# Turning the normalised tiles of a transformer layer's fused pass by DMA instead of TensorE

## The reference

```python
h  = layernorm(x)                       # source norm
Q, K = elu(h@Wq + bq) + 1, elu(h@Wk + bk) + 1;  v = h@Wv + bv
KV = sum_s K[s] v[s]^T  per head (16 heads of 64)
Z  = 1 / (Q . sum_s K[s] + 1e-6)
t  = h + (Q KV Z)@Wo + bo
x1 = layernorm(t)*g1 + be1              # first norm
u  = x1 + gelu(x1@W1 + b1)@W2 + b2      # hidden size 4096
xa = x + layernorm(u)*g2 + be2          # second norm
n  = layernorm(xa)                      # third norm
out = xa + n@weight.T + pooled(n)@disha # folded into n@Wf
```

## Time and profile before

| | us |
|---|---|
| Median of 3 runs | 1622.37 (1622.12 to 1623.51) |
| The profiled execution's own time | 1624.31 |
| Its span, core 5, the slowest | 1622.8 (other cores from 1617.1) |
| TensorE busy | 1539.5 (95%) |
| VectorE busy | 928.4 (57%) |
| ScalarE busy | 598.4 (37%) |
| GpSimd busy | 502.7 (31%) |
| Granted TensorE clock, mean | 0.982 |

### The profile page before, as it was taken

How to read it: one execution, slowest core, us unless ns; L and a number is a source line. 1 busy time by engine, 2 the same in 40 slices (tenths; PEclk the granted TensorE clock), 3 DMA queues, 4 the chain that set the end, 5 groups by cost and what they waited for, 6 DMA issues and landing times.

```text
span 1622.8 us, 28100 instructions; the slowest of 8 cores (1617.1 to 1622.8 us)
## 1 busy us (share of the span) xinstructions
PE 1539.5 (95%) x9892; PEld 928.7 (57%) x9892; DVE 928.4 (57%) x1042; ACT 598.4 (37%) x1010; POOL 502.7 (31%) x438
## 2 busy tenths in 40 slices
PE   2699999999789999999999999999999999999995
PEld 1254544554356666666666666666666666666662
DVE  1466665665626574756657474755657475665314
ACT  1244555544533233333323333342323333332321
POOL 3464544545344222222222222222122222222101
PEclk9799999999899999999999999999999999999998
DMA  9776655457772201111110201111120111111011
GB/s 174 180 169 181 158 161 142 131 138 160 146 148 93 74 32 66 39 54 53 53 66 27 79 27 66 45 48 53 53 78 27 66 40 53 53 53 54 26 40 39
DMA packets 52183, 135.60 MB, mean 84 GB/s; under 512 B 5968, under 2 KB 14160, under 8 KB 52048
## 3 DMA queue, kind: packets, MB, share of 16 engines
q1 hardware_dynamic: 31408, 101.82, 18.7%
q0 software_dynamic: 14112, 25.70, 10.5%
q10 hardware_dynamic: 6528, 6.29, 1.3%
HBM read 117.53 MB, written 41.94 MB: 98 GB/s over the span
## 4 chain that ended last, share of the span: by engine, by line
PE 92%; issue 2%; DVE 2%; DMA 2%; POOL 1%; ACT 1%; SPq 0%; DVEq 0%; ACTq 0%; POOLq 0%
PE psH L1100 27%; PE psY L1081 27%; PE psY L444 13%; PE psS L673 7%; PE psS L493 6%; PE psS L415 6%; PE psS L659 1%; PE psS L547 1%; PE psH L423 1%; DMA qt_s<-arena 1%; PE psS L436 1%; PE psS L568 1%; DMA arena<-x 1%; PE psY L415 1%; PE psY L493 0%
## 5 line engine op out<-in xcount | busy, mean ns | idle before, releaser
L1100 PE MATMUL psH<-arena 128*128 128x256 bf16 x4096 | 531.6, 273 | 1.4 <-ACT arena L558 1.4
L1081 PE MATMUL psY<-arena 128*128 128x512 bf16 x2048 | 525.8, 379 | 0.4 <-DVE arena L601 0.4
L1006 ACT ACTIVATE arena<-psH,arena 128x256 bf16<-128x256 f32 x512 | 243.4, 475 | 733.3 <-PE psH L1100 731.4
L1100 PEld LDWEIGHTS psH<-arena 128*128 128x128 bf16 x4096 | 398.5, 98 | 131.0 <-issue 1.6
L1081 PEld LDWEIGHTS psY<-arena 128*128 128x128 bf16 x2048 | 200.3, 98 | 133.7 <-issue 1.6
L444 PE MATMUL psY<-arena 128*128 128x512 bf16 x1024 | 236.5, 386 | 16.3 <-DMA arena<-Wk 10.1
L589 DVE RECIPROCAL arena<-arena 128x512 f32<-128x512 f32 x56 | 187.4, 3346 | 29.8 <-ACT arena L579 29.8
L444 PEld LDWEIGHTS psY<-arena 128*128 128x128 bf16 x1024 | 100.2, 99 | 135.1 <-issue 25.6
L680 DVE TENSOR_TENSOR arena<-psS,arena 128x512 f32<-128x512 f32 x64 | 44.1, 689 | 168.1 <-PE psS L673 168.1
L502 DVE TENSOR_TENSOR arena<-psS,arena 128x512 f32<-128x512 f32 x60 | 41.3, 689 | 151.6 <-PE psS L493 151.4
L673 PE MATMUL psS<-arena 128*128 128x512 bf16 x512 | 122.2, 383 | 2.6 <-ACT arena L668 2.6
(11 more groups left out here) (113 smaller groups left out, 1479.7 us busy)
## 6 DMA issues: line engine op xcount, KB each, us to landing
arena<-x SPq DMA_DIRECT2D x64, 512.0 KB, 4.3
xb_s<-arena SPq DMA_DIRECT2D x32, 512.0 KB, 3.4
arena<-W POOLq DMA_DIRECT2D x64, 256.0 KB, 5.3
arena<-xb_s SPq DMA_DIRECT2D x32, 512.0 KB, 3.2
out<-arena SPq DMA_DIRECT2D x32, 512.0 KB, 2.9
arena<-qt_s SPq DMA_DIRECT2D x16, 512.0 KB, 3.2
qt_s<-arena ACTq DMA_DIRECT2D x24, 256.0 KB, 5.2
arena<-WfT SPq DMA_DIRECT2D x16, 256.0 KB, 2.9
```

The costliest lines, as they stand in the source:

```text
L1006: sc.activation(hT[n % 3][:, :], hbank[n % 2], AF.Gelu, bias=b1c[:, c:c + 1]).then_inc(b_g, 1)
L1081: ii = te.matmul(ybank[k], hT[n % 3][:, (k // 2) * P:(k // 2 + 1) * P], w2_v[c][:, (k % 2) * HALF:(k % 2 + 1) * HALF], start=(c == 0), sto ...
L1100: ii = te.matmul(hbank[n % 2], w1_v[c // NCH][:, w, (c % NCH) * P:(c % NCH + 1) * P], x1T[i % 2][:, w, :], start=(w == 0), stop=(w == NCH ...
```

## The change

For pairs 2 to 15 the output of the first norm, and for pairs 0 to 14 that of the third, is turned by a transposing DMA on SP's queue, from `nb` straight into `x1T` or `nT`. The 8 transposes on TensorE and the copy on ScalarE go for these. Pairs 0 and 1 keep them for the first norm, pair 15 for the third. Waits that went by the transposes (`b_tx`, `b_tn`, `b_nT`) go by the DMAs' semaphores `s_tx` and `s_tn`.

The side jobs stand behind other steps: `final` of half 0 behind 12 and 13 (before 10 and 11), attention of half 1 behind 14 and 15 (before 16 and 17), `final` of half 1 behind 16 and 17 (before 14 and 15), `den` behind 20, 21, 23, 25 (before 21, 22, 24, 26). All four kinds alternate between bank 0 and bank 1. On ScalarE `src_norm` moves from behind gelu 11 to 13, `x1_cast` from 14 and 22 to 16 and 21, `den_out` from 21, 23, 25, 27 to 20, 22, 24, 26. On VectorE the two `o_add` of half 1 go behind `x1` of half 1. On SP `q_in` goes ahead of the stores, and a turn stands ahead of `x_in`, ahead of `q_in`, and on both sides of the stores.

The diff, cut to its core:

```diff
+        s_tx, s_tn = [sema("x1T0"), sema("x1T1")], [sema("nT0"), sema("nT1")]
...
         def x1_cast(sc, j, sub):
             sc.wait_ge(b_x1, 2 * j + sub + 1)
-            if sub == 1:
-                sc.wait_ge(b_tx, 2 * j + 1)
-            elif j >= 2:
-                sc.wait_ge(b_tn, 2 * (j - 1))
-            elif j == 1:
-                sc.wait_ge(b_tx, 2)
+            if j >= 2:
+                if sub == 1:
+                    sc.wait_ge(s_tx[0], 16 * (j - 1))
+                else:
+                    sc.wait_ge(s_tn[1], 16 * (j - 1))
+            elif 2 * j + sub >= 1:
+                sc.wait_ge(b_tx, 2 * j + sub)
...
+        def x1_turn(sy, j, sub):
+            sy.wait_ge(b_x1b, 2 * j + sub + 1)
+            sy.wait_ge(b_h, NFCH * (j - 1))
+            sy.dma_start_transpose(x1T[j % 2][:, :, sub * P:(sub + 1) * P], nb[:, :]
+                                   ).then_inc(s_tx[sub], 16)
+
+        def n_turn(sy, j, sub):
+            sy.wait_ge(b_n, 2 * j + sub + 1)
+            if 4 * j + 2 * sub > 0:
+                sy.wait_ge(b_wf, 4 * j + 2 * sub)
+            sy.dma_start_transpose(nT[:, :, :], nb[:, :]).then_inc(s_tn[sub], 16)
...
         def n_norm(v, j, sub):
             n = 2 * j + sub + 1
             v.wait_ge(b_rx, n)
-            if sub == 0:
-                v.wait_ge(b_tx, min(2 * j + 4, 2 * NSUP))
+            if sub == 1 and j == NSUP - 1:
+                v.wait_ge(b_tn, 1)
+            elif sub == 1:
+                v.wait_ge(s_tn[0], 16 * (j + 1))
+            elif j == 0:
+                v.wait_ge(b_tx, 4)
             else:
-                v.wait_ge(b_tn, 2 * j + 1)
+                v.wait_ge(s_tx[1], 16 * min(j, NSUP - 2))
...
         def final(te, j, sub, nh, bank):
-            te.wait_ge(b_nT, 2 * j + sub + 1)
+            if j == NSUP - 1:
+                te.wait_ge(b_nT, sub + 1)
+            else:
+                te.wait_ge(s_tn[sub], 16 * (j + 1))
...
                 sy.wait_ge(b_xa, 2 * i - 1)
                 xb_in(sy, i - 1, 1)
+                n_turn(sy, i - 1, 0)
                 if i + 1 < NSUP:
                     sy.wait_ge(b_xa, 2 * i)
                     x_in(sy, i + 1, 1)
+                n_turn(sy, i - 1, 1)
+                if i + 2 < NSUP:
+                    sy.wait_ge(b_at, 4 * (i + 2))
+                    q_in(sy, i + 2)
+                if i + 1 < NSUP:
+                    x1_turn(sy, i + 1, 0)
                 o_store(sy, i - 1, 0)
                 o_store(sy, i - 1, 1)
+                if i + 1 < NSUP:
+                    x1_turn(sy, i + 1, 1)
             if i + 2 < NSUP:
                 if i >= 1:
                     sy.wait_ge(s_out[0], 16 * i)
                 x_in(sy, i + 2, 0)
-                if i >= 1:
-                    sy.wait_ge(b_at, 4 * (i + 2))
-                    q_in(sy, i + 2)
                 sy.wait_ge(b_qh, 4 * (i + 1))
...
-                if c == 9 and post:
-                    n_out(sc, i - 1, 0, sbf[0])
-                if c == 11 and pre and post:
+                if c == 13 and pre and post:
                     src_norm(sc, i + 1, 1)
-                if c == 13 and post:
-                    n_out(sc, i - 1, 1, sbf[1])
-                if c == 14 and pre:
+                if c == (16 if post else 14) and pre:
                     x1_cast(sc, i + 1, 0)
-                if c == 19 and pre:
-                    x1_out(sc, i + 1, 0, sbf[0])
+                if c == 19 and not post:
+                    x1_out(sc, 1, 0, sbf[0])
...
-                o_add(v, i - 1, 0, 0, sbank[1])
-                o_add(v, i - 1, 0, 1, sbank[0])
-                o_add(v, i - 1, 1, 0, sbank[0])
-                o_add(v, i - 1, 1, 1, sbank[1])
+                o_add(v, i - 1, 0, 0, sbank[0])
+                o_add(v, i - 1, 0, 1, sbank[1])
             if pre:
                 t_add(v, i + 1, 1, 0, sbank[0])
                 t_add(v, i + 1, 1, 1, sbank[1])
                 t_stats(v, i + 1, 1)
                 x1(v, i + 1, 1)
+            if post:
+                o_add(v, i - 1, 1, 0, sbank[0])
+                o_add(v, i - 1, 1, 1, sbank[1])
```

More of the change, by code:

```diff
@@ L552, in x1_out @@
             sc.wait_ge(b_tx, 2 * j + sub + 1)
-            if j >= 2:
-                sc.wait_ge(b_h, NFCH * (j - 1))
-            elif j == 1:
+            if j == 1:
                 sc.wait_ge(s_qst[0], 32 * NG)
@@ L1007, in act_b @@
                               bias=b1c[:, c:c + 1]).then_inc(b_g, 1)
-                if c == 9 and post:
-                    n_out(sc, i - 1, 0, sbf[0])
-                if c == 11 and pre and post:
+                if c == 13 and pre and post:
                     src_norm(sc, i + 1, 1)
-                if c == 13 and post:
-                    n_out(sc, i - 1, 1, sbf[1])
-                if c == 14 and pre:
+                if c == (16 if post else 14) and pre:
                     x1_cast(sc, i + 1, 0)
-                if c == 19 and pre:
-                    x1_out(sc, i + 1, 0, sbf[0])
-                if c == 21 and far:
-                    den_out(sc, i + 2, 0, sbank[1])
-                if c == 22 and pre:
-                    x1_cast(sc, i + 1, 1)
[L1022 to L1026, removed]
+                if c == 19 and not post:
+                    x1_out(sc, 1, 0, sbf[0])
+                if c == 20 and far:
+                    den_out(sc, i + 2, 0, sbank[0])
+                if c == 21 and pre:
+                    x1_cast(sc, i + 1, 1)
+                if c == 22 and far:
+                    den_out(sc, i + 2, 1, sbank[1])
+                if c == 24 and not post:
+                    x1_out(sc, 1, 1, sbf[1])
+                if c == 24 and far:
                     den_out(sc, i + 2, 2, sbank[0])
-                if c == 27 and far:
+                if c == 26 and far:
                     den_out(sc, i + 2, 3, sbank[1])
@@ L1092, in pe_b @@
                 n = NFCH * i + c
-                if c == 0:
+                if c == 0 and i < 2:
                     te.wait_ge(b_xT, 2 * i + 2)
+                elif c == 0:
+                    te.wait_ge(s_tx[0], 16 * (i - 1))
+                    te.wait_ge(s_tx[1], 16 * (i - 1))
                 if i == 0 and c % NCH == 0:
@@ L1114, in pe_b @@
                     attn(te, i + 1, 0, 1, sbank[1])
[L1115 to L1119, removed]
+                if c == 12 and post:
+                    if pre:
+                        te.wait_ge(b_t, 4 * (i + 1) + 1)
+                    else:
+                        te.wait_ge(b_o, 4 * (i - 2) + 3)
+                    if i == 1:
+                        te.wait_ge(b_ws, 16)
+                    final(te, i - 1, 0, 0, sbank[0])
@@ L1120, in pe_b @@
+                if c == 13 and post:
                     if pre:
                         te.wait_ge(b_t, 4 * (i + 1) + 2)
[L1122 to L1131, removed]
-                    final(te, i - 1, 1, 0, sbank[0])
@@ L1133, in pe_b @@
-                if c == 15 and post:
-                    final(te, i - 1, 1, 1, sbank[1])
-                if c == 16 and pre:
-                    te.wait_ge(b_t, 4 * (i + 1) + 1)
+                    else:
+                        te.wait_ge(b_o, 4 * (i - 2) + 4)
+                    final(te, i - 1, 0, 1, sbank[1])
+                if c == 14 and pre:
+                    if post:
+                        te.wait_ge(b_o, 4 * (i - 1) + 1)
+                    else:
+                        te.wait_ge(b_t, 4 * (i + 1) + 1)
+                    attn(te, i + 1, 1, 0, sbank[0])
@@ new lines, in pe_b @@
+                if c == 15 and pre:
+                    if post:
+                        te.wait_ge(b_o, 4 * (i - 1) + 2)
+                    else:
+                        te.wait_ge(b_t, 4 * (i + 1) + 2)
+                    attn(te, i + 1, 1, 1, sbank[1])
+                if c == 16 and post:
+                    if pre:
+                        te.wait_ge(b_t, 4 * (i + 1) + 3)
+                    else:
+                        te.wait_ge(b_o, 4 * (i - 1) + 1)
+                    final(te, i - 1, 1, 0, sbank[0])
@@ L1137, in pe_b @@
+                if c == 17 and post:
+                    if pre:
+                        te.wait_ge(b_t, 4 * (i + 1) + 4)
+                    else:
+                        te.wait_ge(b_o, 4 * (i - 1) + 2)
+                    final(te, i - 1, 1, 1, sbank[1])
+                if c == 18 and not post:
+                    te.wait_ge(b_t, 4 * (i + 1) + 3)
+                    x1_tr(te, 1, 0, sbf[0])
+                if c == 20 and far:
+                    te.wait_ge(s_q, 16 * (i + 2))
                     if post:
@@ L1138, in pe_b @@
                         te.wait_ge(b_o, 4 * (i - 1) + 3)
-                    attn(te, i + 1, 1, 0, sbank[0])
-                if c == 17 and pre:
-                    te.wait_ge(b_t, 4 * (i + 1) + 2)
+                    else:
+                        te.wait_ge(b_xT, 3)
+                    den(te, i + 2, 0, sbank[0], b_den)
+                if c == 21 and far:
```

(20 more changed lines are left out.)

6 lines of the change are left out of this document (2 added, 4 removed).

## The result

The changed kernel takes 1596.24 us in the median of 4 runs against 1622.24 of the kernel before; the ratio is 0.9835, 95% interval 0.9816 to 0.9855.

What follows compares the result with a forecast made beforehand. TensorE's streamed columns bound the fused pass; 25.9 us of transposes plus 1.1 of late starts, less 0 for stalls, take 27.0 from 1622.4, giving 1595.4 us. Range 1592 to 1630, the forecast's own 1592 to 1600.

Steps and rivals of the forecast that it cites:

- TensorE's saving: In the fused pass, 58 transpose groups and late starts leave TensorE: 27.0 us in all, 1.8 per iteration over 15.
- the late starts: Third-norm transpose groups that start late since normed rows come just in time: 1.1 us, upper bound 4.1.
- the term of the groups: 58 groups of 8 transposes removed from TensorE's steps, 0.447 us each: 25.9 us.
- X: Time from the last write of nb to the turned data being visible: 5.0 us, ends 2.9 and 9.5.
- the qt_s row: Profile row of a 256 KB DMA from SP in short runs of 256 bytes, landing in 5.0 us.
- the estimate of 10.5 us: Rule against the forecast: a turn as eight 128x128 tiles in a row takes 10.5 us, total time 1681 us.
- The covers: Slack between nb or nT being ready and the third-norm turn's use: 7.0 us first half, 8.3 second.
- the formula: TensorE's stall per iteration when turns outlast their slack: (X - 7.0) + (X - 8.3).
- Rival A: Turn's eight blocks pass one behind another; TensorE stalls at final matmuls, slower beyond X = 8.55; 1651 us at 9.5; chance 0.21.
- The tight chain: Denominators' ring: last x1 step to 46.3, store lands 50.6, den_out due 50.9; margin 0.3 us, cost taken 0.
- Rival C: Turns hold o_store of half 1 by 2 us, den_out blocks the gelus: 9 us lost, 1604; chance 0.04.
- Rival D: More DMA writes slow TensorE's steps beyond 1.737 us; no size given; no chance of its own, others 0.02.

## Why the prediction was right

**TensorE's saving.** Forecast 0.447 us per group and 27.0 in all with the late starts. Iterations 1 to 14 together went from 1008.8 to 982.8 us (519.37 to 1528.16 before, 517.08 to 1499.84 after): 26.0, where 14 x 1.79 and the late starts give 26.1. Putting 60 groups back restored the old time, so the term of the groups is shown and not only summed. The late starts can be read off the iterations before: one of 72.36 and three of 72.27 or 72.28 where the rule is 72.05, 1.0 in all against 1.1 forecast; in the changed kernel all are 70.26.

**The total.** The medians of the runs differ by 26.0 us, those of the cores' spans by 27.5, and from the start of iteration 0 to the end the median core is 26.4 us shorter (1169.4 and 1143.0). The forecast of 27.0 lies among them, and the interval of the ratio, 23.5 to 29.8 us, can't tell them apart. The ends vary more than that from core to core: iteration 0 takes 65.2 to 66.2 us before and 65.3 to 66.6 after. So the agreement of 1596.24 with 1595.4 to 0.8 us is in part luck.

**The turn's time.** Forecast X = 5.0 from the qt_s row, with ends of 2.9 and 9.5; measured 3.0 to land and 3.2 with the hop. This step was off, on the cautious side: the row of plain transfers was the near one, 2.9 us for the same 256 KB. Since both lie under the covers, the time did not depend on it.

The Trainium skill says in "Advanced Engine Details and Errata", section "X-Bar Transpose (TRN2)", that turning DMAs are as fast as regular ones. The trace agrees with it, 3.0 against 2.9 us. It does not agree with the estimate of 10.5 us that takes eight tiles in a row at the 1309 ns of "VectorE: DVE Perf Modes", section "The three transpose paths", in the same Trainium skill.

**The covers.** 7.0 and 8.3 us were worked out from steps alone, less 0.2 for hops between engines that no row was given for; the traces show 0.15 from nb complete to the issue and 0.13 from the landing to the use. Turns of about 5 us for both halves, of 8.6 and 7.5, and of 10.8 and 9.8 made TensorE wait 0, 1.5 and 4.8 us per iteration, against 0, 1.6 and 5.3 by the formula; the iteration grew by 0, 1.7 and 6.6. Rival A had its mechanism right and its condition wrong: no turn in one DMA takes that long. Its prices were too low for long turns, since they had neither the slow matmuls behind a stall nor the shorter room of the last iteration in them.

**What I left out.** The prediction took one X. Landings vary from 3.0 to 4.7 us for the third norm and to 5.0 for the first, and the slowest core counts; that is why the new places matter, and no step of mine named it.

**The tight chain.** It came out within 0.2 us. Time line of the changed kernel, 1048 us on (the iteration starts at 1008.89):

```profile
1049.79 2.12 POOL L543 TENSOR_TENSOR arena<-arena 128x1024 f32<-128x1024 f32 x1 [8.08 <-ACT arena L539]
1049.88 3.12 DVE L523 SCALAR_TENSOR_TENSOR arena<-arena 128x1024 f32<-128x1024 f32 x1
1051.12 5.68 SPq L704 DMA_DIRECT2D out<-arena  x2
1051.88 1.20 POOL L515 TENSOR_SCALAR arena<-arena 128x1 f32<-128x1 f32 x1
1053.23 0.57 POOL L518 TENSOR_TENSOR arena<-arena 128x1 f32<-128x1 f32 x1
1053.90 1.28 DVE L527 SCALAR_TENSOR_TENSOR arena<-arena 128x1024 f32<-128x1024 f32 x1 [0.90 <-POOL arena L518]
```

x1 of half 1 ends at 1055.18, 46.3 us in, as forecast; den_out starts at 1059.71, 50.8 in, against a forecast of 50.9. The row of 3.12 us on VectorE is longer than the 1.28 the sum had, and still ends before t_rstd does. Rival C's wait occurs once in the whole pass, 0.7 us of ScalarE for the store to out, and the iterations show none of it. Rival D: steps stay at 1.74 us with the DMA share up from 0.15 to 0.23.

## What to carry to other kernels

When one engine is busy the whole of a stage, price an edit by what it takes off that engine, read from the distances between starts, and put dummy work back to prove it. A transfer that replaces work on that engine is free exactly as long as its latency, taken at its slowest and not at its median, fits between the producer's end and the consumer's turn; count that room in steps before looking at bandwidth. At the start and the end of a program, where nothing covers it or the queues are full, keep the short path.

## What the runs showed of the hardware

A turning DMA of 128x1024 bf16 from SBUF to SBUF lands in 3.0 us at the median, up to 5.0 in the pass, and holds SP for 1.24 us; a quarter of it lands in 2.3, and the whole so costs 0.7 us more than the quarter. Its row in the page's list of packets shows it as many small ones: packets under 512 B rose from 5968 to 67216 (58 turns, about 1056 each), and the steps of the pass still take 1.74 us.

GpSimd can hold VectorE up: the group of x1's first step (line 522 before, 523 after; out and in as in the earlier trace rows) had a mean of 1287 ns and now 2110, since in the pass that step of half 1 starts 0.09 us after b2_add of half 0 and takes 3.12 us; the step of half 0, which meets no b2_add, takes 1.28. In one iteration b2_add had started 0.46 us ahead, and the step took 2.75: it ends about 1.1 us after b2_add does each time. GpSimd's own time is unchanged, 2.13 us at the median before and after. A turn is in flight beside both halves' steps, so it is not the cause. All this was hidden and cost nothing here.

```profile
L523 DVE SCALAR_TENSOR_TENSOR arena<-arena 128x1024 f32<-128x1024 f32 x32 | 67.5, 2110 | 1.7
```

A stall of TensorE can cost more than its length: after 3.5 us idle the next eight matmuls ran at a clock of 0.50 and took 3.57 us instead of 1.89, and in the kernel with such stalls in each iteration the mean granted clock was 0.961 to 0.968 on six cores. After 3.3 us idle in the tail, six cores fell to 0.50 and two stayed at 1.00, with the same kernel.
